# Dot and cross products of the gathered vectors on VectorE instead of GpSimd, in the last stage of a four-layer graph network

## The chip, the core and the metric

One Trainium2 chip, one of its cores. The metric is the device time of one execution of the whole program in microseconds. One core has a matrix engine (TensorE; PE, and PEld for its weight loads), a vector engine (VectorE; DVE), a scalar engine (ScalarE; ACT), GpSimd (POOL) and SyncE (SP), which only issues transfers here.

## The reference

12,500 nodes with 32 features, and 412,500 directed edges that are sorted by their destination. Four graph layers follow one another, each with a residual sum and a layer norm. The change touches the fourth layer alone:

```python
src, dst = (edge_index[0], edge_index[1])
R = jax.nn.relu(abs_distances[:, None] @ w1 + b1) @ w2 + b2      # 384 radial weights an edge
Y = spherical_harmonics(rel_vec)
Fj = features[src]                                               # gathered rows: 8 scalars, 8 vectors
...
acc = acc + _NORM[i] * jnp.einsum('euv,ef,evi,ofi->euo', Rb[..., k], Yf, Fb, C)
...
out = out.at[dst].add(msg)
```

`features` is x after three layers, `abs_distances` the edge weight, `rel_vec` a direction with three components. Of each gathered node the 32 features are 8 scalars and 8 vectors of three. With the real coupling tensors the sum falls into a few kinds of terms: scalars, vectors, the dot product of each vector with the unit direction, the cross product of each vector with it, and the direction times a weighted sum.

## The kernel before

The program runs in this order: preparation, a stage over all edges for layer 1 that also builds an adjacency image (`edges_and_adjacency`), ten propagation steps on that image and layer 3 (`propagate`), and the last stage, `tensor_messages`. That one takes the edges in NG = 324 groups of 10 tiles of 128 edges. Groups alternate between two sets of buffers (`m` = 0 or 1). The programs of the engines are written out by hand and meet at semaphores; a loop turn (`Fori`) is one pair of groups. For group n:

- SP loads edge weights, destinations and unit directions (`load`, L1551 to L1553). For group n this waits until the rows of group n-2 are ready (`rows_ready`), so a load starts when VectorE finishes a group. The indices are loaded separately (L1543).
- GpSimd gathers the source nodes by ten indirect transfers of one tile each (`gather`, L1500), and after the gather of group n+1 it makes the products of group n (`features`, L1503 to L1522): three multiplications of 128x240 elements (`pool_t`), one addition, one subtraction and one more addition, which write dot products and cross products into `m_features`. It waits for `loaded` and for ScalarE's `copied`, and signals `features_ready`.
- ScalarE makes the hidden radial layer (L1586), copies the gathered features into `m_features` and into `f1_cyclic`, the vectors with two components repeated (L1592 to L1595, signals `copied`), and builds the one-hot matrix of destinations (L1603, L1607).
- TensorE makes the radial weights, 384 an edge, in five batches of two tiles (`radial`, L1631), and sums the messages into the 128 nodes of a block with the one-hot matrix (`product`, L1636). The product of group n-1 is done within group n: tile 0 after batch 1, the nine others after batch 4. A group whose edges reach into a second block of nodes needs one more pass of ten tiles for it (`further_visits`).
- VectorE (`group`, L1756 to L1789) waits for `features_ready`, multiplies the radial weights of each batch by the features (L1766 once, L1770 three times a batch), drains its pipeline (L1774), sums (L1775), adds a finished block (`add`, L1730 and L1733), makes the one-hot matrix of a second block where there is one (L1737), sums again (L1778), keeps the destinations (L1783), and completes the rows (L1785, L1789), which signals `rows_ready`.

A batch buffer of the radial weights is one of two halves: TensorE may write batch b once VectorE has used batch b-2 (`r_used`).

Of the kernel before, what the change touches and what calls it, by code (L numbers as in the profile page):

```python
# [21 lines left out]
F32 = mybir.dt.float32  # L22
# [4 lines left out]
ALU = mybir.AluOpType  # L27
ACT = mybir.ActivationFunctionType
AX = mybir.AxisListType
# [6 lines left out]
EP = P  # L36
G = 10
# [3 lines left out]
NG = E // GE  # L41
PAIRS = NG // 2
# [39 lines left out]
def view(ap, offset, dims):  # L82

    return bass.AP(ap.tensor, ap.offset + offset, [list(ap.ap[0])] + [list(d) for d in dims])
# [13 lines left out]
def await_alone(eng, passed, sem, value):  # L98


    eng.wait_ge(sem, value)
    eng.sem_inc(passed, 1)
# [1317 lines left out]
def tensor_messages(nc, k, s):  # L1420
# [6 lines left out]
    sb, pb, sem, io = k.sb, k.pb, k.sem, k.io  # L1427
    U = 8
# [14 lines left out]
    unit = [sb(f"m_unit{m}", [EP, G, 5], F32, s) for m in range(2)]  # L1443

    FX = 8 * U
    feat = [sb(f"m_features{m}", [EP, G, FX], F32, s) for m in range(2)]
    cyclic = [sb(f"f1_cyclic{m}", [EP, G, U, 5], F32, s) for m in range(2)]
    pool_t = [sb(f"pool_t{n}", [EP, G, U, 3], F32, s) for n in range(3)]


    RW = 2 * U + 1
# [16 lines left out]
    loaded = [sem(f"m_loaded{m}") for m in range(2)]  # L1468
    idx_loaded = [sem(f"m_idx_loaded{m}") for m in range(2)]
    gathered = [sem(f"m_gathered{m}") for m in range(2)]  # L1470
    hid_ready, r_ready, r_used = sem("m_hid_ready"), sem("m_r_ready"), sem("m_r_used")
    copied, pool_step, features_ready = sem("m_copied"), sem("m_pool_step"), sem("m_features_ready")
    rows_ready, features_used = sem("m_rows_ready"), sem("m_features_used")
    extra_ready, rows_free = sem("m_extra_ready"), sem("m_rows_free")
    product_done, added = sem("m_product_done"), sem("m_added")
# [12 lines left out]
    with ExitStack() as q:  # L1488
        r_ps = pb("radial_ps", [EP, 2, RB, 512], F32, q)
        v_ps = pb("m_visit_ps", [P, 3, 512], F32, q)  # L1490
        with nc.Block() as block:

            @block.gpsimd
            def _(pool):
                def gather(i, m, first):
                    await_alone(pool, k.passed_pool, idx_loaded[m], (i + 1) * 16)
                    if not first:
                        await_alone(pool, k.passed_pool, copied, i * 2 + (m - 1))
                    for j in range(G):
                        pool.indirect_dma_start(src[m][:, j, :], None, k.x3_d,  # L1500
                                                bass.IndirectOffsetOnAxis(idx[m][:, j:j + 1], 0)).then_inc(gathered[m], 16)

                def features(n, turn, m, first):  # L1503

                    mul = lambda to, a, b: nc.gpsimd.tensor_tensor(to, a, b, ALU.mult).then_inc(pool_step, 1)
                    shifted = lambda at: view(cyclic[m][:], at, [[5 * U, G], [5, U], [1, 3]])
                    r_o = lambda at: view(unit[m][:], at, [[5, G], [0, U], [1, 3]])
                    await_alone(pool, k.passed_pool, loaded[m], turn * 48)
                    if not first:
                        await_alone(pool, k.passed_pool, features_ready, n)  # L1510
                    await_alone(pool, k.passed_pool, copied, n + 1)
                    mul(pool_t[0][:], shifted(0), r_o(0))
                    mul(pool_t[1][:], shifted(2), r_o(1))
                    mul(pool_t[2][:], shifted(1), r_o(2))
                    part = lambda i: view(pool_t[0][:], i, [[3 * U, G], [3, U]])
                    s_out = view(feat[m][:], U, [[FX, G], [1, U]])
                    await_alone(pool, k.passed_pool, pool_step, n * 5 + 3)
                    nc.gpsimd.tensor_tensor(s_out, part(0), part(1), ALU.add).then_inc(pool_step, 1)
                    nc.gpsimd.tensor_tensor(view(feat[m][:], 3 * U, [[FX, G], [1, U], [2 * U, 3]]), pool_t[1][:], pool_t[2][:],
                                            ALU.subtract).then_inc(pool_step, 1)  # L1520
                    await_alone(pool, k.passed_pool, pool_step, n * 5 + 5)
                    nc.gpsimd.tensor_tensor(s_out, s_out, part(2), ALU.add).then_inc(features_ready, 1)  # L1522
                gather(0, 0, True)
                gather(0, 1, True)
                features(0, 1, 0, True)
                with pool.Fori(1, PAIRS) as i:
                    gather(i, 0, False)
                    features(i * 2 - 1, i, 1, False)
                    gather(i, 1, False)
                    features(i * 2, i + 1, 0, False)  # L1530
                features(NG - 1, PAIRS, 1, False)

            @block.sync
            def _(sp):
# [155 lines left out]
            def _(dve):  # L1690
                tt, ts, red = nc.vector.tensor_tensor, nc.vector.tensor_scalar, nc.vector.tensor_reduce
# [47 lines left out]
                def visits(m, drained=False):  # L1739
# [5 lines left out]
                    with dve.If(end - block > 1):  # L1745
                        with dve.Fori(block + 1, end) as b:
# [6 lines left out]
                            dve.reg_add(extra_used, extra_used, 3)  # L1753
                            dve.reg_add(count, count, 1)

                def group(i, m, first):  # L1756
                    n = i * 2 + m
                    fe = feat[m][:]
                    dve.wait_ge(features_ready, n + 1)
                    if not first:  # L1760
                        dve.wait_ge(rows_free, n - 1)
                    for b in range(NBAT):
# [16 lines left out]
                    table_first, table_end = blocks(dve, n)  # L1779
                    dve.reg_mov(first_r, table_first)  # L1780
                    dve.reg_mov(end_r, table_end)
                    dve.wait_ge(loaded[m], (i + 1) * 48)
                    nc.vector.tensor_copy(kept[m][:], dst[m][:])  # L1783
                    dve.drain()  # L1784
                    tt(view(turned_along[:], 0, [[3 * U, G], [U, 3], [1, U]]), view(along[:], 0, [[U, G], [0, 3], [1, U]]),  # L1785
# [52 lines left out]
```

## Time and profile before

| | |
|---|---|
| median of 3 runs | 15099.62 us |
| lowest and highest | 15078.14 and 15099.76 us |
| span of the profiled execution | 18914.5 us |
| busy in it: PE, DVE, ACT, POOL | 14494.5, 10873.1, 5258.0, 7506.3 us |
| last stage in it, from 12619 to 18871 us | 6252 us for 324 groups |

The profiled execution is 3815 us longer than the median of the undisturbed runs. Its durations and orders are what can be read; how the difference is spread over the stages the profile does not say. In the rows below, times are microseconds from the start of the span, a row of a timeline merges equal instructions that follow each other ("x3"), and what stands in brackets is the time for which the engine stood idle before, with what ended it. "issue" means that nothing in the profile explains the idle time, "remote" that a semaphore moved and no recorded instruction moved it. PE work is listed by its matmul instructions, two for one tile in this type.

### The profile page before, as it was taken

To read this page: it belongs to the slowest core of one execution; us is meant where nothing else is said; L and a number is where in the kernel's file an instruction comes from. 1 tells how busy PE (TensorE), PEld (TensorE's weight loads), DVE (VectorE), ACT (ScalarE), POOL (GpSimd) and SP (SyncE) were. 2 spreads that over 40 slices of the span, in tenths; PEclk is the share of its full clock that TensorE was granted. 3 is DMA by queue.
4 is the path that set the end of the run, shared out by engine and by line. 5 is a ranking of instruction groups with operands and counts; after the bars stand their busy time and mean duration, and the time that the engine had idled before them with its cause. 6 is when DMAs were issued, how large, how long until landed. Compare 5 with 4: busy or idle time off the path is not lost. (4 is left out here: it accounts for less than half of the span.)

```text
span 18914.5 us, 402579 instructions
## 1 busy us (share of the span) xinstructions
PE 14494.5 (77%) x139778; PEld 9671.3 (51%) x139779; DVE 10873.1 (57%) x15415; ACT 5258.0 (28%) x10677; POOL 7506.3 (40%) x8530
## 2 busy tenths in 40 slices
PE   2666666666666666799999999977787778777877
PEld 2555555555555555655555555544444444444444
DVE  6444444444444444455555555557787777777777
ACT  2333333333333333100000000014444444444443
POOL 4444444444444444000000000026676666666765
PEclk8666666666666666699999999989999999999999
DMA  2100010101010010165666566541111111111111
GB/s 72 23 21 22 21 22 20 23 20 23 21 23 21 21 23 21 60 190 187 190 188 190 188 191 190 171 122 27 27 28 28 28 27 28 28 27 27 28 27 27
DMA packets 1143323, 1240.77 MB, mean 66 GB/s; under 512 B 399134, under 2 KB 1111834, under 8 KB 1142394
## 3 DMA queue, kind: packets, MB, share of 16 engines
q1 hardware_dynamic: 932485, 1124.29, 19.8%
q0 software_dynamic: 210496, 113.01, 4.2%
q14 instruction: 259, 2.11, 0.0%
q8 instruction: 83, 1.36, 0.0%
HBM read 1143.04 MB, written 93.60 MB: 65 GB/s over the span
## 5 line engine op out<-in xcount | busy, mean ns | idle before, releaser
L1500 POOL DMA_INDIRECT m_src<-x_after_layer,m_idx x3240 | 3130.8, 966 | 6032.8 <-DMA m_idx<-in_src 4921.4
L180 POOL DMA_INDIRECT l_xin<-in_x,l_idx x3240 | 3095.0, 955 | 4382.1 <-DMA l_idx<-in_src 3211.4
L1232 PE MATMUL p_prod<-a_slot,f_parts 128*32 128x448 fp8e4 x90552 | 4318.4, 353 | 105.4 <-DVEq L1397 50.6
L1232 PEld LDWEIGHTS p_prod<-a_slot,f_parts 128*32 128x32 bf16 x90552 | 2428.9, 97 | 1932.8 <-issue 115.6
L1631 PE MATMUL radial_ps<-radial_w,radial_hidden 128*128 128x384 f32 x6480 | 2598.2, 538 | 719.1 <-DVE m_products L1770 420.0
L581 PE MATMUL a_ps<-hot_hi,hot_lo 128*128 128x196 bf16 x6272 | 1640.4, 303 | 1902.7 <-ACT a_image L680 958.9
L749 DVE TENSOR_TENSOR hot_hi<-window_hi,number_ps 128x1568 bf16<-128x1568 f32 x784 | 1401.2, 1787 | 2895.4 <-PE degree_ps L582 1502.9
L1636 PE MATMUL m_visit_ps<-m_products,m_onehot 128*128 128x288 f32 x8420 | 2445.4, 440 | 561.8 <-DVE m_onehot L1737 261.8
L1636 PEld LDWEIGHTS m_visit_ps<-m_products,m_onehot 128*128 128x128 f32 x8420 | 1669.8, 201 | 1370.3 <-issue 767.9
L1631 PEld LDWEIGHTS radial_ps<-radial_w,radial_hidden 128*128 128x128 f32 x6480 | 1212.8, 202 | 1992.9 <-issue 793.3
L680 ACT ACTIVATE a_image<-a_ps 128x392 fp8e4<-128x392 f32 x3136 | 1478.5, 496 | 2644.6 <-PE a_ps L581 1672.3
L1314 DVE TENSOR_SCALAR a_slot<-a_nibbles 128x1568 int32<-128x1568 int32 x1085 | 1059.3, 976 | 1953.6 <-PE p_prod L1232 992.0
L581 PEld LDWEIGHTS a_ps<-hot_hi,hot_lo 128*128 128x128 bf16 x6272 | 720.3, 115 | 2339.5 <-issue 1133.7
L1770 DVE TENSOR_TENSOR m_products<-radial_ps,m_features 128x256 f32<-128x256 f32 x4860 | 1745.6, 415 | 0.0
L1766 DVE TENSOR_TENSOR m_products<-radial_ps,m_features 128x512 f32<-128x512 f32 x1620 | 1113.6, 687 | 1078.0 <-PE radial_ps L1631 453.5
L582 PE MATMUL degree_ps<-hot_hi,hot_lo 128*128 128x196 bf16 x6272 | 1659.5, 306 | 9.1 <-issue 9.0
L1603 ACT ACTIVATE m_difference<-m_nodes,m_dst 128x128 f32 x3240 | 982.9, 389 | 2459.3 <-PEq L1656 1590.6
L622 PE MATMUL e_visit_ps<-e_onehot,e_hidden 128*97 x8420 | 1369.8, 335 | 352.5 <-ACT e_hidden L693 169.9
L622 PEld LDWEIGHTS e_visit_ps<-e_onehot,e_hidden 128*97 128x97 f32 x8420 | 1313.7, 216 | 426.7 <-issue 420.0
L611 PE MATMUL h_ps<-w1a,xt 49*128 49x96 f32 x6480 | 1271.1, 357 | 262.6 <-issue 132.8
L611 PEld LDWEIGHTS h_ps<-w1a,xt 49*128 49x128 f32 x6480 | 1127.5, 260 | 451.0 <-issue 450.8
L1270 ACT ACTIVATE turned<-p_prod,digit_weight 128x448 f32<-128x448 f32 x154 | 97.7, 635 | 4254.0 <-PE p_prod L1232 4254.0
(203 smaller groups left out, 12640.4 us busy)
## 6 DMA issues: line engine op xcount, KB each, us to landing
a_nibbles<-multiplicity_digit SPq DMA_DIRECT2D x1085, 784.0 KB, 4.4
edge_w<-in_edge_weight SPq DMA_DIRECT2D x324, 320.0 KB
multiplicity_digit<-a_packed SPq DMA_DIRECT2D x392, 196.0 KB
l_xin<-in_x,l_idx POOLq DMA_INDIRECT x3240
m_src<-x_after_layer,m_idx POOLq DMA_INDIRECT x3240
xt<-in_edge_attr SPq DMA_DIRECT2D x324, 80.0 KB, 2.2
edge_directions<-rel_unit SPq DMA_DIRECT2D x12, 675.0 KB
m_unit<-edge_directions SPq DMA_DIRECT2D x324, 25.0 KB
```

Of the source, the lines that this page charges most:

```text
L180: pool.indirect_dma_start(k.xin[m][:, j, :], None, k.io["x"], bass.IndirectOffsetOnAxis(k.idx[m][:, j:j + 1], 0)).then_inc(k.gathered[m], 16)
L581: counts = nc.tensor.matmul(a_ps[:, bank, v * WC:(v + 1) * WC], lo, hot_hi[batch % 2][:, w, :], start=True, stop=True)
L582: mm = nc.tensor.matmul(degree_ps[:, 0:WC], lo, hot_hi[batch % 2][:, w, :], start=False, stop=False, skip_group_check=True)
L611: mm = nc.tensor.matmul(h_ps[:, t * DH:(t + 1) * DH], xt[:, m % 2, (b * HT + t) * EP:(b * HT + t + 1) * EP], w1a[:], start=True, stop=True)
L622: mm = nc.tensor.matmul(visit_ps[:, 0:P], hid[m % 2][:, j, :], view(onehot[:], (v % 2) * (G * P) + j * P, [[1, P]]), start=(j == 0), stop= ...
L680: nc.scalar.activation(view(image[:], h * (NB * QW) + 4 * l, [[QW, NB], [1, 4]]).bitcast(FP8), view(a_ps[:], l % 2 * 512, [[1, NB], [NB, 4 ...
L749: tt(hot_hi[b % 2][:], view(k.window_hi[:, bass.ds(at, WB)], 0, [[1, WB], [0, WC]]), view(numbers, 0, [[0, WB], [1, WC]]), ALU.is_equal)
L1232: mm = nc.tensor.matmul(view(prod[rows, w, :], 0, [[QW, 2], [1, QW]]), source[:, h * HH + j, r * D:(r + 1) * D], slots[h][:, 2 * w:2 * w + ...
L1500: pool.indirect_dma_start(src[m][:, j, :], None, k.x3_d, bass.IndirectOffsetOnAxis(idx[m][:, j:j + 1], 0)).then_inc(gathered[m], 16)
L1631: mm = nc.tensor.matmul(r_ps[:, half, t, 0:RD], hid[m][:, b * RB + t, :], w2[:], start=True, stop=True)
L1636: mm = nc.tensor.matmul(view(v_ps[:], (v % 3) * 512, [[U + 1, D], [1, U + 1]]), onehot[one][:, j, :], view(prod[m][:], j * PW + FIRST, [[R ...
L1770: mul = tt(view(prod[m][:], t0 * PW + LONG + o * U * RW + 1, [[PW, RB], [RW, U], [1, 2 * U]]), view(r_ps[:], at + 4 * U * U, [[512, RB], [ ...
```

## The change

GpSimd's `features` and its semaphores (`pool_step`, `features_ready`) are gone; GpSimd only gathers. VectorE has a function `features` of five instructions and two drains, called at the head of each group after waits for `loaded` and `copied`. The sum of three products is one reduction instead of two additions. The wait for `loaded` further down in the group is gone, since it now stands at the head.

```diff
@@ GpSimd
-                def features(n, turn, m, first):
-                    mul = lambda to, a, b: nc.gpsimd.tensor_tensor(to, a, b, ALU.mult).then_inc(pool_step, 1)
-                    ...
-                features(0, 1, 0, True)
                 with pool.Fori(1, PAIRS) as i:
                     gather(i, 0, False)
-                    features(i * 2 - 1, i, 1, False)
                     gather(i, 1, False)
-                    features(i * 2, i + 1, 0, False)
-                features(NG - 1, PAIRS, 1, False)
@@ VectorE
+                def features(m):
+
+                    shifted = lambda at: view(cyclic[m][:], at, [[5 * U, G], [5, U], [1, 3]])
+                    r_o = lambda at: view(unit[m][:], at, [[5, G], [0, U], [1, 3]])
+                    tt(turned_f[0][:], shifted(0), r_o(0), ALU.mult)
+                    tt(turned_f[1][:], shifted(2), r_o(1), ALU.mult)
+                    tt(turned_f[2][:], shifted(1), r_o(2), ALU.mult)
+                    dve.drain()
+                    red(view(feat[m][:], U, [[FX, G], [1, U]]), turned_f[0][:], AX.X, ALU.add)
+                    tt(view(feat[m][:], 3 * U, [[FX, G], [1, U], [2 * U, 3]]), turned_f[1][:], turned_f[2][:], ALU.subtract)
+                    dve.drain()
+
                 def group(i, m, first):
                     n = i * 2 + m
                     fe = feat[m][:]
-                    dve.wait_ge(features_ready, n + 1)
+                    dve.wait_ge(loaded[m], (i + 1) * 48)
+                    dve.wait_ge(copied, n + 1)
+                    features(m)
                     if not first:
                         dve.wait_ge(rows_free, n - 1)
...
                     dve.reg_mov(end_r, table_end)
-                    dve.wait_ge(loaded[m], (i + 1) * 48)
                     nc.vector.tensor_copy(kept[m][:], dst[m][:])
```

## Rows read from the trace of the kernel before

**Rows 1.** The stage's stretch: length, each engine's busy time (instructions), clock, DMA share, GB/s

```profile
12619.00:18871.00 6252.00, 4958.87 (x14884) 2878.36 (x14884) 4874.98 (x9049) 2654.98 (x5184) 4310.97 (x5184) 0.93 0.14 27
```

**Rows 2.** Waits in the stage's stretch: who for whom, us in total, times, longest

```profile
POOL pool_t L1505 <- ACT f_cyclic L1595: 626.2, 159, 13.7
DVE m_products L1766 <- PE radial_ps L1631: 453.5, 277, 7.0
DVE m_products L1766 <- issue: 294.8, 126, 5.4
DVE m_products L1766 <- remote: 273.8, 103, 7.7
PE m_visit_ps L1636 <- DVE m_onehot L1737: 261.8, 97, 6.6
```

**Rows 3.** Timeline of VectorE, second half of a group with one block, and next head

```profile
15040.03 0.69 DVE L1766 TENSOR_TENSOR m_products<-radial_ps,m_features 128x512 f32<-128x512 f32 x1
15040.64 1.08 DVE L1770 TENSOR_TENSOR m_products<-radial_ps,m_features 128x256 f32<-128x256 f32 x3
15041.84 1.49 DVE L1775 TENSOR_REDUCE m_along<-m_products 128x80 f32<-128x1280 f32 x1
15043.25 0.45 DVE L1730 TENSOR_REDUCE m_visit<-m_visit_ps 128x32 f32 x1
15043.86 0.19 DVE L1733 TENSOR_TENSOR m_sums<-m_sums,m_visit 128x32 f32 x1 [0.17 <-issue]
15044.35 2.82 DVE L1778 TENSOR_REDUCE m_products<-m_products 128x320 f32<-128x2560 f32 x1 [0.30 <-issue]
...
15047.33 0.41 DVE L1785 TENSOR_TENSOR m_turned_along<-m_along,m_unit 128x240 f32<-128x240 f32 x1
15047.81 0.58 DVE L1789 TENSOR_TENSOR m_products<-m_products,m_turned_along 128x240 f32<-128x240 f32 x1
15048.31 0.68 DVE L1766 TENSOR_TENSOR m_products<-radial_ps,m_features 128x512 f32<-128x512 f32 x1
...
15049.90 0.68 DVE L1766 TENSOR_TENSOR m_products<-radial_ps,m_features 128x512 f32<-128x512 f32 x1
```

**Rows 4.** Timeline of VectorE after groups with a second block: one-hot, next heads

```profile
15021.97 1.49 DVE L1737 TENSOR_TENSOR m_onehot<-m_dst_kept,m_nodes 128x1280 f32<-128x1280 f32 x1 [0.55 <-issue]
...
12747.60 0.69 DVE L1766 TENSOR_TENSOR m_products<-radial_ps,m_features 128x512 f32<-128x512 f32 x1 [3.67 <-issue]
...
18840.80 0.69 DVE L1766 TENSOR_TENSOR m_products<-radial_ps,m_features 128x512 f32<-128x512 f32 x1 [4.05 <-PE radial_ps L1631]
```

**Rows 5.** Timeline of TensorE: the extra pass of that group and what follows

```profile
15023.96 5.33 PE L1636 MATMUL m_visit_ps<-m_products,m_onehot 128*128 128x288 f32 x20 [2.65 <-DVE m_onehot L1737]
15030.03 2.84 PE L1631 MATMUL radial_ps<-radial_w,radial_hidden 128*128 128x384 f32 x8 [0.74 <-issue]
```

**Rows 6.** Groups by line and shape, 13400 to 18800 us: busy, mean ns, idle before

```profile
L1733 DVE TENSOR_TENSOR m_sums<-m_sums,m_visit 128x32 f32 x367 | 121.9, 332 | 61.0 <-issue 61.0
L1737 DVE TENSOR_TENSOR m_onehot<-m_dst_kept,m_nodes 128x1280 f32<-128x1280 f32 x85 | 134.6, 1584 | 26.4 <-issue 15.4 <-PE m_visit_ps L1636 10.5
```

**Rows 7.** Durations by line, ns: least, median, most; L1785 and L1505 from 13400 to 18800 us

```profile
L1785 DVE TENSOR_TENSOR m_turned_along<-m_along,m_unit x281: 407/409/475, 13407.9 to 18784.4; 128x240 f32<-128x240 f32 x141
L1505 POOL TENSOR_TENSOR pool_t<-f_cyclic,m_unit x843: 681/707/2024, 13418.4 to 18796.1; 128x240 f32<-128x240 f32 x169
L1733 DVE TENSOR_TENSOR m_sums<-m_sums,m_visit x420: 191/193/1301, 12684.1 to 18866.2; 128x32 f32 x140
```

**Rows 8.** Timeline of GpSimd: a whole turn, first and last of ten gathers

```profile
15042.37 0.98 POOL L1500 DMA_INDIRECT m_src<-x_after_layer,m_idx  x1 [0.46 <-issue]
...
15053.86 0.95 POOL L1500 DMA_INDIRECT m_src<-x_after_layer,m_idx  x1 [0.30 <-DMA m_unit<-edge_directions]
15057.76 2.04 POOL L1505 TENSOR_TENSOR pool_t<-f_cyclic,m_unit 128x240 f32<-128x240 f32 x3 [2.95 <-ACT f_cyclic L1595]
...
15061.14 0.38 POOL L1522 TENSOR_TENSOR m_features<-m_features,pool_t 128x80 f32<-128x80 f32 x1 [0.18 <-POOL m_features L1519]
15062.47 0.99 POOL L1500 DMA_INDIRECT m_src<-x_after_layer,m_idx  x1 [0.94 <-issue]
```

**Rows 9.** Timeline of ScalarE: last copy for the group that starts at 15048.31

```profile
15037.61 0.36 ACT L1595 COPY f_cyclic<-m_src 128x160 f32<-128x160 f32 x1
```

More of the change, by code:

```diff
@@ L1447, in tensor_messages @@
     cyclic = [sb(f"f1_cyclic{m}", [EP, G, U, 5], F32, s) for m in range(2)]
-    pool_t = [sb(f"pool_t{n}", [EP, G, U, 3], F32, s) for n in range(3)]
+    turned_f = [sb(f"turned_f{n}", [EP, G, U, 3], F32, s) for n in range(3)]
     RW = 2 * U + 1
@@ L1471, in tensor_messages @@
     hid_ready, r_ready, r_used = sem("m_hid_ready"), sem("m_r_ready"), sem("m_r_used")
-    copied, pool_step, features_ready = sem("m_copied"), sem("m_pool_step"), sem("m_features_ready")
+    copied = sem("m_copied")
     rows_ready, features_used = sem("m_rows_ready"), sem("m_features_used")
@@ L1501, in gather @@
                                                 bass.IndirectOffsetOnAxis(idx[m][:, j:j + 1], 0)).then_inc(gathered[m], 16)
-                def features(n, turn, m, first):
-                    mul = lambda to, a, b: nc.gpsimd.tensor_tensor(to, a, b, ALU.mult).then_inc(pool_step, 1)
[L1506 to L1522, printed above, removed]
                 gather(0, 0, True)
                 gather(0, 1, True)
-                features(0, 1, 0, True)
                 with pool.Fori(1, PAIRS) as i:
                     gather(i, 0, False)
-                    features(i * 2 - 1, i, 1, False)
                     gather(i, 1, False)
-                    features(i * 2, i + 1, 0, False)
-                features(NG - 1, PAIRS, 1, False)
             @block.sync
```

## The prediction

> **What bounds the kernel now.** I read the windows first, then the waits, then the timelines. The change touches only the last stage, 6252 us of the profiled span for 324 groups, 19.3 us a group. In it PE is busy 79%, DVE 78%, POOL 69% [rows 1]: three engines are nearly full, and the shares don't say which one sets the pace.
>
> The cycle of each, without waits, does. VectorE: a batch takes 1.59 us (15049.90 - 15048.31), and there are four; the last batch with its drain takes 1.81 (15041.84 - 15040.03); L1775 1.41; the adding of a block 1.10 (15044.35 - 15043.25); L1778 to the next head 3.96 (15048.31 - 15044.35). Together 14.6 us [rows 3]. A second block costs it about 3.2 more (a one-hot of 1.49 us with its gaps, and a second adding of about 1.1), and 97 of the 324 groups have one [rows 2, 4], so 15.6 us on average. GpSimd: the ten gathers take 12.44 us (15053.86 + 0.95 - 15042.37), the products 3.76 (15061.14 + 0.38 - 15057.76), the step to the next gather 0.94: 17.1 us [rows 8]. That is more than VectorE's, but its products wait another 626 us, 1.9 us a group, for ScalarE's copies [rows 2], so in this execution GpSimd isn't the bound.
>
> What VectorE waits for at the heads of groups decides the matter. I measured from the end of each L1789 to the start of the next L1766. In the 226 intervals after a group without a second block the mean is 0.1 us, 24 us in all; [rows 3] show one, where the head follows at once. In the 97 after a group with one the mean is 3.66 us, none is under 1.0 and 90 are over 2.3; first 3.67, last 4.05 [rows 4]. Their cause is TensorE: the extra one-hot is made late on VectorE, TensorE waits for it, runs 5.33 us, and only then makes the first radial weights of the next group [rows 5]. So in seven heads of ten VectorE sets the pace, and in three TensorE.
>
> **The change part by part.** *Added on VectorE.* Three multiplications of 128x240. L1770 x3 shows what such a series costs: 1.08 us for three of 256 elements, of which the first two steps take (1.08 - 0.41)/2 = 0.33 each; a step that ends in a drain takes 0.48, as L1785 (15047.81 - 15047.33) [rows 3]. That gives 0.33 + 0.33 + 0.48 = 1.14 us. The reduction of 240 elements to 80: no row shows it; I take the step of 0.33, bounded above by 0.45, the reduction L1730. The subtraction writes with a stride as L1789 does, 0.58, or takes 0.41 as L1785. Behind it comes a drain, and the sequencer must then take up the waits for `rows_free` and `r_ready`: after L1733 such a passage cost 0.30 [rows 3]. I take 0.83 for the two. Sum 1.14 + 0.33 + 0.83 = 2.3 us a group. Bounds: five steps of 0.33 without a cost of the drains, 1.65; five of 0.58, 2.9. The chosen value is nearest to rows with the same shape and the same drain.
>
> *Where it counts.* In 226 groups nothing covers it: 226 x 2.3 = 520 us. In 97 it lies in the wait for TensorE and costs about 5 us in all (seven heads under 2.3). That cover holds because the whole of group n, its one-hot of the second block too, moves with VectorE, and TensorE's lag behind it stays as it is. If the cover were gone, 97 x 2.3 = 223 us more. Within the group nothing absorbs the delay: batches 0 and 1 wait ready in both halves, and later batches wait for `r_used`, which moves too.
>
> *Removed from GpSimd.* 3.76 us a group of 17.1, and the chain from copies over products to the head. On VectorE this gives back the wait for `features_ready`: in heads with no second block before them at most the 24 us above. In the others it hid in TensorE's time.
>
> *Less collision.* L1733 takes 193 ns in the median and up to 1301 [rows 7], 332 in the mean [rows 6]; L1737 1.49 alone [rows 4] and 1.584 in the mean [rows 6]. Both read two inputs from SBUF, and by their start times 156 of the 158 L1733 over 250 ns overlap a product of GpSimd. Gone: 423 x 0.139 + 97 x 0.09 = 68 us.
>
> *Moved waits.* `loaded` and `copied` at the head: the last copy for the group that starts at 15048.31 is over at 15037.97 [rows 9], 10 us before. While such a wait lasted, all of VectorE's group, `r_used` and `rows_ready` would be queued behind it, and TensorE and SP's loads would wait for those; with 10 us of slack I cost it at nothing. The gather of group n+2 still starts at `copied` of group n, and earlier than now, since no products stand before it. The removed wait at L1783 had long been met: nothing.
>
> *GpSimd undisturbed.* The undisturbed runs are 3815 us shorter than this execution. If VectorE and TensorE run more freely there, GpSimd's 17.1 us come closer to being the bound, and removing 3.76 of them gives something back. The rows show only that it is near. Bounds: 0, and 1.5 us (17.1 - 15.6) in 226 groups, 340 us. I take 45, near zero, since the heads without a second block show almost no wait.
>
> Sum: 520 + 5 - 24 - 68 - 45 = +388 us, which is 19,300 on the profiled span of 18,914.5. On the undisturbed median: 15,099.6 + 388, rounded 15,490. I add the same microseconds there, since all added work is VectorE's own. A difference of 0.2%, 30 us, is about what a measurement of this kernel can tell from no change.
>
> **A rule against the change.** L1785, the nearest instruction to the new ones (two inputs in SBUF, 240 elements), ran beside GpSimd's gathers at 407 to 475 ns in all 281 records [rows 7, 8]: no gather delays it. The Trainium skill, SBUF — State Buffer, section "SBUF: two separate sides", says that GpSimd and a VectorE instruction with two SBUF inputs exclude each other on shared ports when the GpSimd operation reads SBUF, whichever starts first holding them for its whole length. If a gather counted as such an operation, the four new two-input instructions would each be held up; the trace does not show it.
>
> **The rivals.** (A) Faster: undisturbed, GpSimd is the bound. Its cycle then is 17.1 plus the wait for copies, up to 19.0; after the change VectorE sets 15.6 + 2.3 = 17.9, less 0.2 for collisions. From a present undisturbed cycle of 17.7 on, the change gains; at 18.4, in the middle, it gives 0.7 x 324 = 230, so 14,870. For it: 17.1 is above 15.6, and TensorE's waits may be shorter undisturbed. Against: heads without a second block show 0.1 us of wait. (B) TensorE sets the pace in far more groups than the heads show, since VectorE waits 1022 us in all at L1766 [rows 2], 355 + 24 of them at the heads counted above; the 643 us within groups, 2.0 us a group, might take up much of the delay. That gives 0 to half of the sum, 15,100 to 15,290. Against: a wait within the group comes from a batch that itself waits for `r_used`. (C) No cover: the extra one-hot comes later and TensorE's wait, 262 us in 97 groups now, grows with it; all 324 groups pay, 745 - 137 = +608, so 15,710. (D) Locking: each of four new instructions is held for half a gather of 0.95 us, in 226 groups 4 x 0.48 x 226 = 434 more, 15,920. It is the outcome of the rule above. (E) The change moves work, but VectorE's new work is hidden everywhere: this is (B) at its lower end.
>
> **How the numbers follow.** Forecast 0.64, between 15,300 and 15,650 by the bounds of 1.65 and 2.9 us. (A) 0.12, (B) 0.14, half of it within 30 us, (C) 0.07, (D) 0.03. The range of 15,180 to 15,710 leaves out A, D and the lower end of B, under 2 in 10. Faster 0.12, same 0.07, slower 0.81.
>
> **What the profile after would show.** Five new lines on VectorE at each head, 2.3 us from first start to L1766 in groups after a one-block group; head waits for TensorE shorter by that much after the others, about 1.3 us left; L1733 near 193 ns in the mean; POOL's share down by some 1250 us; the stage near 6640 us of the span. If the new instructions take over 0.5 us each, (D) holds; if the waits for TensorE at L1766 stay as long after groups with a second block, (C); if the stage grows by less than 150 us and waits within groups shrink, (B). I am wrong in sign if the stage is shorter.

## The result, and the profile after

| | median, us | lowest to highest | last stage, us | granted clock in it |
|---|---|---|---|---|
| before | 15097.29 | 15078.14 to 15099.76 | 5574 (run e0_before) | 0.98 |
| after | 15829.74 | 15825.21 to 15834.63 | 6346 | 0.90 |

The change makes the kernel slower, ratio 1.049 (95% interval 1.0475 to 1.0505), by 732 us. I had forecast 388 us. The sign was right; the size was half of what it came to, and the time lies outside my range of 15,180 to 15,710.

The profile shown ahead of the prediction was of a disturbed execution, 18,914 us long (one of the ten runs of e0_before, at 24,264 us, was disturbed too); a profile of the same kernel on an undisturbed one (e0_before, span 15,086.8 us) takes its place in every comparison below.

The last stage from its first to its last message instruction, first after, then e0_before. The columns are those of [rows 1]:

```profile
9441.00:15787.00 6346.00, 5080.71 (x14872) 2966.11 (x14872) 5412.22 (x10652) 2644.85 (x5172) 3155.76 (x3227) 0.90 0.15 27
```

```profile
9469.00:15043.00 5574.00, 4728.33 (x14872) 2733.69 (x14872) 4884.71 (x9037) 2647.72 (x5160) 4285.66 (x5158) 0.98 0.16 31
```

The stage grew by 772 us; everything ahead of it and behind it together took 28 us less. VectorE has 528 us more to do and GpSimd 1130 less. TensorE has the same 14,872 instructions and is busy for 352 us more. Its clock has two levels, 1.2 and 2.4 GHz; a mean grant of 0.98 means that 4% of the stage passed at the lower one, 0.90 that 19% did. By the clock intervals in the two traces that is 201 us before and 1212 after.

After: VectorE from the end of one group to its third batch, at a head with no second block before it. Answers to [rows 3]:

```profile
12016.89 0.58 DVE L1778 TENSOR_TENSOR m_products<-m_products,m_turned_along 128x240 f32<-128x240 f32 x1
12017.50 0.41 DVE L1736 TENSOR_TENSOR turned_f<-f_cyclic,m_unit 128x240 f32<-128x240 f32 x1
12017.82 0.40 DVE L1737 TENSOR_TENSOR turned_f<-f_cyclic,m_unit 128x240 f32<-128x240 f32 x1
12018.14 0.40 DVE L1738 TENSOR_TENSOR turned_f<-f_cyclic,m_unit 128x240 f32<-128x240 f32 x1
12018.62 0.40 DVE L1740 TENSOR_REDUCE m_features<-turned_f 128x80 f32<-128x240 f32 x1
12018.94 0.55 DVE L1741 TENSOR_TENSOR m_features<-turned_f 128x240 f32<-128x240 f32 x1
12019.74 0.69 DVE L1756 TENSOR_TENSOR m_products<-radial_ps,m_features 128x512 f32<-128x512 f32 x1 [0.25 <-issue]
...
12021.34 0.68 DVE L1756 TENSOR_TENSOR m_products<-radial_ps,m_features 128x512 f32<-128x512 f32 x1
...
12024.38 0.69 DVE L1756 TENSOR_TENSOR m_products<-radial_ps,m_features 128x512 f32<-128x512 f32 x1 [1.37 <-PE radial_ps L1607]
```

The new work takes 2.24 us from first start to the first batch (12017.50 to 12019.74). Then, at batch 2, VectorE waits 1.37 us for TensorE: that is new. TensorE in the same group, after:

```profile
12014.32 2.84 PE L1607 MATMUL radial_ps<-radial_w,radial_hidden 128*128 128x384 f32 x8 [0.73 <-issue]
12017.92 0.77 PE L1612 MATMUL m_visit_ps<-m_products,m_onehot 128*128 128x288 f32 x2 [0.75 <-DVE m_products L1778]
12021.48 6.20 PE L1607 MATMUL radial_ps<-radial_w,radial_hidden 128*128 128x384 f32 x12 [2.79 <-DVE m_products L1760]
```

and in e0_before:

```profile
12014.43 0.77 PE L1636 MATMUL m_visit_ps<-m_products,m_onehot 128*128 128x288 f32 x2 [0.75 <-DVE m_products L1789]
12015.86 3.15 PE L1631 MATMUL radial_ps<-radial_w,radial_hidden 128*128 128x384 f32 x8 [0.67 <-DVE m_products L1770]
12019.20 1.56 PE L1631 MATMUL radial_ps<-radial_w,radial_hidden 128*128 128x384 f32 x4 [0.19 <-DVE m_products L1770]
```

Before, TensorE stood idle for 0.67 us ahead of batch 2, did batches 2 and 3 in 3.15 us and batch 4 in 1.56. After, it stood idle for 2.79 us, since both halves were full and VectorE was making features, and then the same twelve instructions took 6.20 us. Over the groups after a one-block group, 224 of 226 with complete records, the wait ahead of batch 2 went from 0.60 to 2.64 us in the median, and that ahead of tile 0 stayed at 1.07 and 1.06. The granted clock of that stretch, and of a neighbouring one (columns: length, PE busy and instructions, granted clock, DMA share, GB/s):

```profile
12018.00:12025.00 7.00, 4.21 (x8) 0.76 0.32 59
12001.90:12008.00 6.10, 6.06 (x10) 0.51 0.03 3
```

In the second one the clock is at its lower level all through: start to start, matmul instructions of 384 columns lie 0.64 us apart there and 0.32 elsewhere. The Trainium skill, TensorE: Matmul & The Clock Gate, section "HAM oscillation — how this bites in real kernels", describes this pattern, an engine that goes idle between bursts and begins each burst cold. This trace agrees in the pattern: 2.8 us of waiting, then 0.64 us a matmul instruction. It does not agree in the size: the idle stretches that the section blames are longer than these.

The little that the kernel before loses to the lower clock lies mostly elsewhere, in the extra pass for a second block, which follows a wait for the one-hot. At full clock that pass takes 5.33 us [rows 5]; in e0_before 40 of the 97 take over 5.6, like this one:

```profile
9654.45 6.94 PE L1636 MATMUL m_visit_ps<-m_products,m_onehot 128*128 128x288 f32 x20 [2.18 <-DVE m_onehot L1737]
```

Sorted by whether VectorE made the one-hot of a second block in the group before ("after two") or not, mean us of VectorE. The head runs from the end of the last instruction of a group to its first batch, the new work included; the waits are those ahead of batches 2 and 3 (a negative one is an overlap); the rest of the group is not shown:

| | groups | head | batch 2 | batch 3 | whole group |
|---|---|---|---|---|---|
| e0_before, after one block | 226 | 0.09 | 0.13 | -0.05 | 16.78 |
| after, after one block | 226 | 2.17 | 1.28 | 0.46 | 20.24 |
| e0_before, after two | 97 | 3.16 | 0.06 | -0.08 | 18.22 |
| after, after two | 97 | 3.04 | 0.06 | -0.08 | 18.11 |

226 x 3.46 - 97 x 0.11 = 771 us, the whole growth of the stage. Of the 3.46, 2.08 are work at the head and 1.66 are waits for a slow TensorE; the rest of a group gives 0.28 back. The 0.11 come from the extra pass, 5.98 us in the mean before and 5.84 after.

### The profile page after: what moved, and what is told of

The parts are those of the page before. It is cut to its first block and busy times, and to the rows that moved or that the text cites. A ratio compares the mean times of both kernels' runs of the same rounds, so it can differ in the third digit from the quotient of the medians.

```text
span 15830.9 us, 400157 instructions
## 1 busy us (share of the span) xinstructions
PE 13477.7 (85%) x139778; PEld 8853.0 (56%) x139779; DVE 11417.9 (72%) x17035; ACT 5159.2 (33%) x10677; POOL 6467.6 (41%) x6586
## 5 line engine op out<-in xcount | busy, mean ns | idle before, releaser
L1500 POOL DMA_INDIRECT m_src<-x_after_layer,m_idx x3240 | 3175.9, 980 | 8060.4 <-DMA m_idx<-in_src 4922.8
L1607 PE MATMUL radial_ps<-radial_w,radial_hidden 128*128 128x384 f32 x6480 | 2825.9, 585 | 832.3 <-DVE m_products L1760 648.4
L1612 PE MATMUL m_visit_ps<-m_products,m_onehot 128*128 128x288 f32 x8420 | 2339.1, 426 | 437.5 <-DVE m_products L1778 224.4
L1607 PEld LDWEIGHTS radial_ps<-radial_w,radial_hidden 128*128 128x128 f32 x6480 | 1381.8, 226 | 2185.4 <-DVE m_products L1760 1050.5
L1314 DVE TENSOR_SCALAR a_slot<-a_nibbles 128x1568 int32<-128x1568 int32 x1085 | 1058.9, 976 | 1957.4 <-PE p_prod L1232 984.8
L581 PE MATMUL a_ps<-hot_hi,hot_lo 128*128 128x196 bf16 x6272 | 1348.2, 267 | 225.8 <-ACT a_image L680 117.6
L582 PE MATMUL degree_ps<-hot_hi,hot_lo 128*128 128x196 bf16 x6272 | 1342.3, 264 | 0.0
L1562 ACT ACTIVATE radial_hidden<-edge_w,radial_w 64x1280 f32<-64x1280 f32 x324 | 868.3, 2680 | 1014.7 <-DMA m_unit<-edge_directions 981.9
L622 PE MATMUL e_visit_ps<-e_onehot,e_hidden 128*97 x8420 | 1028.6, 278 | 186.7 <-DVE e_total L760 138.9
L611 PE MATMUL h_ps<-w1a,xt 49*128 49x96 f32 x6480 | 963.0, 298 | 194.0 <-ACT xt L687 194.0
L622 PEld LDWEIGHTS e_visit_ps<-e_onehot,e_hidden 128*97 128x97 f32 x8420 | 948.0, 166 | 278.6 <-issue 277.4
L1315 DVE TENSOR_SCALAR a_slot<-a_nibbles 128x1568 int32<-128x1568 int32 x1085 | 1051.9, 969 | 0.0
```

The source lines that it names most:

```text
L581: counts = nc.tensor.matmul(a_ps[:, bank, v * WC:(v + 1) * WC], lo, hot_hi[batch % 2][:, w, :], start=True, stop=True)
L582: mm = nc.tensor.matmul(degree_ps[:, 0:WC], lo, hot_hi[batch % 2][:, w, :], start=False, stop=False, skip_group_check=True)
L622: mm = nc.tensor.matmul(visit_ps[:, 0:P], hid[m % 2][:, j, :], view(onehot[:], (v % 2) * (G * P) + j * P, [[1, P]]), start=(j == 0), stop= ...
L1500: pool.indirect_dma_start(src[m][:, j, :], None, k.x3_d, bass.IndirectOffsetOnAxis(idx[m][:, j:j + 1], 0)).then_inc(gathered[m], 16)
L1607: mm = nc.tensor.matmul(r_ps[:, half, t, 0:RD], hid[m][:, b * RB + t, :], w2[:], start=True, stop=True)
L1612: mm = nc.tensor.matmul(view(v_ps[:], (v % 3) * 512, [[U + 1, D], [1, U + 1]]), onehot[one][:, j, :], view(prod[m][:], j * PW + FIRST, [[R ...
```

## The experiments

Medians of 4 to 10 runs. "One" and "two" are the mean lengths of the groups after one block and after two. "Slow groups" are the groups after one block in which TensorE spent more than 1 us of batches 2 to 4 at the lower clock, out of 224 or 225 with complete records.

| run | time, us | ratio to before (95%) | stage | clock | one | two | slow groups |
|---|---|---|---|---|---|---|---|
| after, for comparison | 15,829.74 | 1.0490 (1.0475 to 1.0505) | 6346 | 0.90 | 20.24 | 18.11 | 222 |
| e0_before | 15,085.90 | 1.0002 (0.9992 to 1.0012) | 5574 | 0.98 | 16.78 | 18.22 | 15 |
| e1_no_products | 15,005.87 | 0.9948 (0.9931 to 0.9964) | 5524 | 0.98 | 16.53 | 18.27 | 8 |
| e2_pe_filler | 15,686.22 | 1.0399 (1.0382 to 1.0416) | 6191 | 0.98 | 18.59 | 20.35 | 0 |
| e3_between5 | 15,854.06 | 1.0512 (1.0494 to 1.0529) | 6367 | 0.93 | 18.95 | 21.33 | 22 |
| e4_split | 15,907.57 | 1.0542 (1.0525 to 1.0560) | 6410 | 0.90 | 20.46 | 18.23 | 224 |
| e5_dot_only | 15,448.97 | 1.0242 (1.0225 to 1.0259) | 5954 | 0.94 | 18.13 | 18.98 | 101 |
| e6_tail | 15,841.61 | 1.0499 (1.0482 to 1.0517) | 6345 | 0.91 | 20.02 | 18.58 | 218 |
| e7_between3 | 15,611.67 | 1.0347 (1.0329 to 1.0364) | 6125 | 0.97 | 18.70 | 19.40 | 14 |
| e8_before_early | 15,031.33 | 0.9963 (0.9950 to 0.9977) | 5512 | 0.98 | 16.91 | 17.26 | 54 |
| e9_after_early | 15,747.90 | 1.0438 (1.0424 to 1.0452) | 6246 | 0.91 | 20.15 | 17.29 | 215 |
| e10_after_early_between3 | 15,485.63 | 1.0263 (1.0247 to 1.0279) | 5986 | 0.99 | 18.54 | 18.36 | 5 |
| e11_before_add_first | 15,199.66 | 1.0072 (1.0058 to 1.0085) | 5662 | 0.96 | 17.83 | 16.67 | 109 |

**e0_before.** No edit.

> The kernel before, unchanged, for a profile of an execution as long as the undisturbed ones: the recorded one is 3815 us longer, that of the changed kernel (15,831 us) is not. Theory 1 (clock): the 732 us are about 520 us of new work on VectorE in groups with nothing to cover it, and the rest comes from TensorE, which now idles 2.6 us while VectorE makes the features, and then runs matmuls at half clock (0.64 us instead of 0.32). It expects in the undisturbed kernel before far less time at half clock in the last stage than the 1251 us after the change, under 900. Theory 2 (work alone): 324 x 2.26 us = 732 us, since no head has a cover when undisturbed; it expects head waits near zero after groups with a second block too, and time at half clock like that after the change. Time about 15,097.

The clock speaks for theory 1: 201 us of the stage at the lower level, not 1212. So do the heads after a second block: 3.16 us of wait, with no products on VectorE, against theory 2's zero. What this profile also corrects is GpSimd. It waits for ScalarE's copies for 39 us in the whole stage, not 626 [rows 2]:

```profile
POOL pool_t L1505 <- ACT f_cyclic L1595: 38.8, 39, 13.0
```

It is full almost without a break, as my 17.1 us a turn suggested: 4286 us of instructions, 1086 of idle time that nothing explains and 116 between its own dependent steps fill 5488 of the 5574 us. The chain of work that ended last passes through it too (L1500 with 12.1% of the stage, L1505 with 4.2%). The profile alone can't say what that is worth; the next run, with its theory 3, measures it.

**e1_no_products.** The products are left out on every engine after the first two groups.

```diff
-                    features(m)
+                    if first:
+                        features(m)
```

> The changed kernel with the dot and cross products left out on every engine after the first two groups (stale values are used; all waits stay). VectorE is then as in the kernel before and GpSimd as after. Theories 1 and 2 both expect the 732 us back: 15,100. If GpSimd's products cost time in the kernel before, this is faster than that kernel by what they cost: theory 3 (GpSimd was near its bound) expects 14,700 to 15,000, from VectorE's cycle of 15.6 us with 1 us of waits against the 17.4 us a group that the kernel before takes undisturbed.

15,006 us, 0.5% under the kernel before. That is all that GpSimd's products cost there, about 75 us, its share of the bound and its collisions with VectorE together. Theory 3 had 14,700 to 15,000 and is missed by 6 us at its small end: the effect is there, and it is small. It lies in the groups after one block (16.53 against 16.78 us); those after two gain nothing (18.27 against 18.22). And VectorE's own products cost 824 us in the changed kernel, more than their length: 323 heads of 2.24 us would be 724, even with no cover at all, which is the most that theory 2 can give.

**e2_pe_filler.** Three matmuls whose result isn't used.

```diff
+                        if b == 1:
+                            for _ in range(3):
+                                nc.tensor.matmul(spare_ps[:, 0:RD], hid[m][:, 0, :], w2[:], start=True, stop=True)
```

> The changed kernel with three more matmuls of 384 columns (1.9 us) on TensorE in each group, into a spare bank, after product tile 0, where it now waits for VectorE. They compute nothing that is used. Theory 1: the clock stays up, the waits at batches 2 and 3 after heads (1.3 + 0.46 us in 226 groups, 393 us) vanish; in the 97 groups after a second block, where TensorE is behind, the filler costs up to 2 us each, 190 us: about 15,630, faster than the changed kernel by 200. Theory 2: work for TensorE can't help: the same time at best, up to 200 us longer: 15,830 to 16,030.

15,686 us: faster by 144 us with 323 x 1.9 us of useless work added to TensorE. The clock is back at 0.98. TensorE in a group after one block:

```profile
12035.11 0.77 PE L1613 MATMUL m_visit_ps<-m_products,m_onehot 128*128 128x288 f32 x2 [1.08 <-DVE m_products L1782]
12035.71 2.10 PE L1653 MATMUL spare_ps<-radial_w,radial_hidden 128*128 128x384 f32 x6
12038.49 1.56 PE L1608 MATMUL radial_ps<-radial_w,radial_hidden 128*128 128x384 f32 x4 [0.68 <-DVE m_products L1764]
```

Batch 2 comes in 1.56 us, at full clock, and VectorE's wait for it falls from 1.28 to 0.06 us. These groups go from 20.24 to 18.59 us (226 x 1.65 = 373 us back). The groups after two blocks, where TensorE is late anyway, pay for the filler: 18.11 to 20.35 (97 x 2.24 = 217 us), 1.7 us of it as a later batch 2 and 0.6 as a slower extra pass. The difference is 156 us, 144 measured. By order and dependence alone, more work on TensorE can't make VectorE wait less for it; the clock can. Theory 2 falls.

**e3_between5.**

```diff
-    BETWEEN = (1, 0, 0)
+    BETWEEN = (5, 0, 0)
```

> The changed kernel with five tiles of the product, not one, between radial batches 1 and 2: TensorE's own work fills the wait that the features made. Theory 1: time at half clock falls as with the filler, and the work is useful, so 15,830 - 393 + at most 97 x 2 = 15,550 to 15,650. Theory 2: order alone changes nothing, 15,830, or more where TensorE comes late with batch 2.

15,854 us: theory 1's number was missed by over 200. The profile shows why:

```profile
12013.29 2.84 PE L1607 MATMUL radial_ps<-radial_w,radial_hidden 128*128 128x384 f32 x8 [0.36 <-issue]
12019.27 3.97 PE L1612 MATMUL m_visit_ps<-m_products,m_onehot 128*128 128x288 f32 x10 [3.14 <-DVE m_products L1778]
12023.04 3.24 PE L1607 MATMUL radial_ps<-radial_w,radial_hidden 128*128 128x384 f32 x8
```

Useful work that is put into the idle time is missing from where it came from. TensorE ends the group four tiles earlier and now waits 3.14 us ahead of the product, and the product is what runs slow (ten instructions in 3.97 us; at full clock they take 2.70). The groups after one block still gain, 20.24 to 18.95, but those after two lose 3.2 us each: 1.8 because batch 2 comes after five tiles, and 1.5 because the extra pass, now behind a wait of 4.1 us for its one-hot, is slow in all 97 (7.30 us against 5.84). -292 + 312 = +20 us; measured +24.

**e4_split.** The three multiplications for the next group stand ahead of the long reduction, the rest stays at the head.

```diff
-                def group(i, m, first):
+                def group(i, m, first, ahead=True):
...
-                    dve.wait_ge(loaded[m], (i + 1) * 48)
-                    dve.wait_ge(copied, n + 1)
-                    features(m)
+                    features_end(m)
...
                         visits(1 - m, drained=True)
+                    if ahead:
+                        dve.wait_ge(loaded[1 - m], (i + 1 + m) * 48)
+                        dve.wait_ge(copied, n + 2)
+                        features(1 - m)
```

Here `features` holds the three multiplications and a drain, `features_end` the reduction, the subtraction and a drain.

> The changed kernel with its new work in two places: the three multiplications for the next group after the adding of a block, ahead of the long reduction, and the reduction to dot products and the subtraction at the head. The same instructions on the same engine, but TensorE's wait of 2.6 us becomes two of about half. Theory 1 (an idle stretch of 2.6 us on TensorE brings half clock behind it): the waits at batches 2 and 3 after heads, 1.28 + 0.46 us in 226 groups against about 0.05 before, go away, while both halves still lie behind the one-hot of a second block and stay covered there. 15,830 - 370 = 15,460 to 15,550. Theory 2 (work alone): 15,830, as the work is the same.

15,908 us, slower than the changed kernel, where I expected 300 less. The form of theory 1 in which one idle stretch of 2.6 us does the harm falls:

```profile
12005.61 0.77 PE L1612 MATMUL m_visit_ps<-m_products,m_onehot 128*128 128x288 f32 x2 [2.35 <-DVE m_products L1782]
12007.89 6.73 PE L1607 MATMUL radial_ps<-radial_w,radial_hidden 128*128 128x384 f32 x12 [1.51 <-DVE m_products L1760]
```

Two waits, 2.35 and 1.51 us, with 0.77 us of work between them, bring the lower clock just as well, in all 224 groups. What was right is the cover: in groups after two blocks both halves stay hidden (18.23 against 18.11).

**e5_dot_only.** The cross products are left out on every engine after the first two groups.

```diff
-                    tt(turned_f[1][:], shifted(2), r_o(1), ALU.mult)
-                    tt(turned_f[2][:], shifted(1), r_o(2), ALU.mult)
+                    if first:
+                        tt(turned_f[1][:], shifted(2), r_o(1), ALU.mult)
+                        tt(turned_f[2][:], shifted(1), r_o(2), ALU.mult)
...
-                    tt(view(feat[m][:], 3 * U, [[FX, G], [1, U], [2 * U, 3]]), turned_f[1][:], turned_f[2][:], ALU.subtract)
+                    if first:
+                        tt(view(feat[m][:], 3 * U, [[FX, G], [1, U], [2 * U, 3]]), turned_f[1][:], turned_f[2][:], ALU.subtract)
```

> The changed kernel with only the dot products made on VectorE (one multiplication, one reduction, two drains) and the cross products left out on every engine after the first two groups. About 1.2 us at the head instead of 2.1. Without any products the kernel took 15,006, with all of them 15,830: 824 us. If the cost were in proportion to the work, 1.2/2.1 of it, 470 us: 15,475. Theory 1: TensorE idles 1.6 us, too short for the clock to fall as often, so only 226 x 1.2 = 270 us: 15,280, and a time at half clock near 200 us, not 1219.

15,449 us, nearer to proportion than to 15,280. The head is 1.07 us in groups after one block; the clock is 0.94, half-way: a smaller fall, not none. Batches 2 to 4 are slow in 101 of 224 groups, such as this one:

```profile
12027.71 0.77 PE L1612 MATMUL m_visit_ps<-m_products,m_onehot 128*128 128x288 f32 x2 [1.11 <-DVE m_products L1780]
12029.94 5.83 PE L1607 MATMUL radial_ps<-radial_w,radial_hidden 128*128 128x384 f32 x12 [1.46 <-DVE m_products L1762]
```

Besides, the groups after two blocks are 0.7 us longer than without products, although their new work is hidden. That too is the clock: the extra pass is slow in 84 of 97 groups (6.72 us in the mean) and in 41 without products (6.01), and the head behind it is longer by just that, 3.93 us against 3.20. One such pass:

```profile
12077.46 6.94 PE L1612 MATMUL m_visit_ps<-m_products,m_onehot 128*128 128x288 f32 x20 [2.18 <-DVE m_onehot L1713]
```

**e6_tail.** All of the new work ahead of the long reduction; otherwise as e4_split, with nothing left at the head.

> The changed kernel with all of its new work, for the next group, after the adding of a block and ahead of the long reduction. TensorE's idle time moves as one piece from behind product tile 0 to ahead of it (0.6 + 2.1 us). Theory 1 in the form that the length of the idle stretch counts and not its place: again 15,750 to 15,850, with slow matmuls now in tile 0 and batch 2. If the place counts (batches 2 and 3 are what VectorE waits for, tile 0 isn't), 15,600 or less. Theory 2: 15,830.

15,842 us. The first form is right: place doesn't count much. TensorE idles 3.3 us (mean) ahead of tile 0 and 0.3 us behind it, and batch 2 is late again (1.17 us).

**e7_between3.** `BETWEEN = (3, 0, 0)`.

> The changed kernel with three product tiles between radial batches 1 and 2. Five tiles had moved the idle time from behind tile 0 (2.6 us) to ahead of it (2.7 us in the median) and it took 15,854 us. Three should split it in two stretches of 1.6 us. Theory 1: half clock goes, the 226 groups give back up to 1.7 us each, and batch 2 comes up to 1 us late in 97 groups: 15,830 - 380 + 97 = 15,550. Theory 2: 15,830 to 15,900.

15,612 us, 218 under the changed kernel and 62 over the forecast: groups after one block gain 1.54 us each, those after two lose 1.29. Two waits again, but with three tiles of work between them:

```profile
12020.87 1.78 PE L1612 MATMUL m_visit_ps<-m_products,m_onehot 128*128 128x288 f32 x6 [1.66 <-DVE m_products L1778]
12024.45 3.15 PE L1607 MATMUL radial_ps<-radial_w,radial_hidden 128*128 128x384 f32 x8 [1.81 <-DVE m_products L1760]
```

Batches 2 and 3 take 3.15 us, full clock. Against e4_split this proves little, since that run has the longer single wait (2.35 us). The run to set beside it is e5_dot_only. In the median TensorE waits there 1.0 us ahead of tile 0 and 1.5 ahead of batch 2, around 0.77 us of work, and 101 of 224 groups are slow; in e7 it waits 2.0 and 1.6 us, around 1.8 us of work, and 14 are. The waits of e7 are longer, and its clock stays up: the length of the waits alone doesn't decide. What differs besides is the work between them. No run here goes further into the rule.

**e8_before_early, e9_after_early and e10_after_early_between3.** The one-hot of a second block is made right behind the last batch. e8 is the kernel before with it, e9 the changed kernel, e10 the changed kernel with `BETWEEN = (3, 0, 0)` too.

```diff
+                def early(m):
+
+                    block, end = dve.snap(first_r, min_val=0, max_val=NB - 1), dve.snap(end_r, min_val=1, max_val=NB)
+                    with dve.If(end - block > 1):
+                        dve.wait_ge(product_done, dve.snap(extra_used, min_val=2, max_val=NG * NB))
+                        one_hot(onehot[2], m, dve.snap(first_r, min_val=0, max_val=NB - 2) + 1).then_inc(extra_ready, 1)
...
+                    if not (first and m == 0):
+                        early(1 - m)
                     dve.drain().then_inc(features_used, 1)
```

> The kernel before (products on GpSimd) with the one-hot matrix of a second block made right behind the last batch and not behind the adding of a block. It tests what the cover in the 97 groups is: TensorE waits 2.26 us for that one-hot, and VectorE waits 3.16 us at the next head for TensorE. If the late one-hot is the cause, the head wait falls to about 0.9 us, 97 x 2.2 = 210 us less: 14,870, faster than either kernel. If TensorE is the bound there by its own work, the time stays at 15,086.

> The same edit in the changed kernel. There the features already lie in that wait, of which only 0.8 us is left at the head (3.04 us less 2.2 of features). If the cover is what I take it for, only this rest can be gained: 97 x 0.8 = 78 us, less what the falling clock then costs in those groups as in the others (up to 1.6 us each, 155 us): 15,750 to 15,900, against 15,830. If cover and clock have nothing to do with it, 210 us as in the kernel before: 15,620.

> The changed kernel with the early one-hot and three product tiles between batches 1 and 2. With three tiles alone it took 15,612; the groups after a second block lasted 19.4 us, of which 3.61 us at the head. Early one-hot takes the wait for TensorE there, 1.4 us in 97 groups, 135 us: 15,480. It would show how near the change can come to the kernel before when TensorE is kept busy.

e8 takes 15,031 us, faster than both kernels, by 0.37% and not by 1.4%. TensorE's wait for the one-hot has given way to another:

```profile
PE m_visit_ps L1636 <- DVE m_sums L1733: 156.0, 97, 2.1
```

TensorE must not write a bank before VectorE has added its old content (`added`), and that comes behind the sum L1775. Heads after two blocks fall from 3.16 to 2.16 us, and the 97 groups give back 93 us. The groups after one block take about 30 of them again (16.78 to 16.91 us): the extra pass is hardly ever slow now, but batches 2 to 4 are in 54 groups and not in 15.

Nor did GpSimd leave much room: 4237 us of instructions, 1089 of unexplained idle time and 115 between its own steps fill 5441 of the 5512 us, and my 14,870 needed a stage of 5360. Whether it held this run back, no run here tells.

e9 gained 82 us: groups after two blocks go from 18.11 to 17.29, the 0.8 us that the features had left uncovered, as forecast, without a loss to the clock there; 17.29 is also what e8 has without the new work (17.26), so the addition is still covered in them.

e10 came at 15,486 (15,480 forecast) with the clock at 0.99. It is the changed kernel with both its troubles mended, and it is still 2.6% behind the kernel before: 400 us more than e0_before, 454 more than e8, which has the early one-hot too.

**e11_before_add_first.** The kernel before, with `visits` ahead of the sum L1775.

```diff
-                    red(along[:], view(prod[m][:], 1, [[PW, G], [RW, U], [1, 2 * U]]), AX.X, ALU.add)
                     if not (first and m == 0):
                         visits(1 - m, drained=True)
+                    red(along[:], view(prod[m][:], 1, [[PW, G], [RW, U], [1, 2 * U]]), AX.X, ALU.add)
```

> The kernel before (products on GpSimd) with the adding of a block, and with it the one-hot of a second block, ahead of the sum L1775 instead of behind it. The early one-hot alone gave 57 us, not 210, since TensorE then waited 1.6 us for the semaphore added, which L1733 moves behind the sum of 1.4 us. Here both come 1.4 us earlier. If those two are all that TensorE waits for in the 97 groups, its wait falls from 2.26 to about 0.9 us and the time by 97 x 1.4 = 136 us, to 14,950. If the wait only changes its cause again, 15,030 to 15,086.

15,200 us, slower, where I had 14,950. The groups after two blocks do what I expected, 18.22 to 16.67 (150 us). The 226 others pay 1.05 us each (237 us). The adding now stands right behind the drain, and VectorE is idle ahead of it 420 times with nothing in the profile to explain it, against 98 times and 43 us in e0_before:

```profile
DVE m_visit L1730 <- issue: 222.3, 420, 0.9
```

That is 0.5 us a group. The other half is the clock again, 0.96 instead of 0.98, 109 slow groups instead of 15, and a wait of 0.59 us at batch 2 that was 0.13. A delay of 0.5 us on VectorE cost twice its length here.

## Why the prediction was wrong in its size

*The new work, 2.3 us a head.* Right: 2.24 us from its first start to the first batch, 2.08 on the head. The pieces answer the rows they were taken from: multiplications 0.40 to 0.41 with steps of 0.32, the one with a drain 0.48, the reduction 0.40, the strided subtraction 0.556.

*226 heads pay, 97 don't.* Right, and the best part of it. The heads after two blocks are 3.04 us long with the new work inside, and were 3.16 without; rival C falls. The cover has two parts: making the one-hot earlier (e8) takes 1.0 us off it, adding the block earlier too (e11) brings it to 1.12, so about 2.0 of the 3.16 us come from VectorE's own order. In e9 the 2.16 that are left still hold the new work.

*Collisions.* Right as durations: L1733, 360 ns in the mean in e0_before, is 198 as L1709; L1737, 1654 ns, is 1494 as L1713. Together 423 x 0.16 + 97 x 0.16 = 83 us of VectorE's time, 68 forecast, though what falls in the groups after two blocks earns nothing, as e1 shows:

```profile
L1709 DVE TENSOR_TENSOR m_sums<-m_sums,m_visit 128x32 f32 x422 | 83.4, 198 | 71.2 <-issue 71.2
L1736 DVE TENSOR_TENSOR turned_f<-f_cyclic,m_unit 128x240 f32<-128x240 f32 x323 | 131.0, 405 | 3.7
```

All 186 of the L1733 in e0_before that take over 281 ns overlap a product of GpSimd, and those beside a gather alone take 193 ns. Rival D falls too: the multiplications take 402 to 405 ns in the mean, 873 of 969 of them beside a gather, and none over 468. So the exclusion that the Trainium skill, SBUF — State Buffer, section "SBUF: two separate sides", states is seen here between VectorE and GpSimd's arithmetic, and not between such a VectorE instruction and a gather.

*GpSimd near its bound.* 45 us for it, 24 for its semaphore and 68 for the collisions, 137 in all; e1_no_products gives 75. Rival A falls: in e0_before GpSimd's turn is as full as I feared, and yet it is worth under 1% of the time.

*"Within the group nothing absorbs the delay … later batches wait for `r_used`, which moves too."* This is the step that failed, and not in the direction that I weighed. I let TensorE shift by 2.3 us at no price. A shift means that it stands idle, for 2.8 us instead of 0.7, and an engine whose clock follows its activity then does the next batches at half speed. VectorE waits for those: 1.28 + 0.46 us instead of 0.13 - 0.05. Term missing from the sum: 226 x 1.66 = 375 us. With the other terms as measured (470 us at the heads, -11 after two blocks, -63 for the rest of a group) it makes the 771. Without it these terms are 396 us, next to my 388. That closeness is partly luck: at the heads I had 525 us where 459 were measured, and I let 137 be given back where it was 63.

There was a hint. [rows 1] give the stage a clock of 0.93, lower than the 0.98 of e0_before, and in the prediction the TensorE row is used for busy shares only. I also took the waits within groups, 2.0 us a group, for something that might *absorb* the delay (rival B). In e0_before they are about 0.1 us: there was nothing there to absorb it, and the question to ask was what TensorE does after it has waited.

The range of 15,180 to 15,710 took its upper end from rival C. Its bounds on VectorE's work were wide enough; a rival with another engine's reaction was missing.

## What to carry to other kernels

Where two engines hand work to each other batch by batch, work added to one can be idle time for the other, and in this kernel idle time on TensorE had a price of its own: count the added stall, look at the granted clock of the stretch behind it, and if it falls, add the slow matmuls that the first engine then waits for. Here 2.1 us at the head cost 3.5. To test for it, give the idle engine work that isn't needed; here the kernel got 144 us faster, which dependences alone can't bring about. And when a wait recurs only after certain groups, sort the heads by it before pricing: the 97 groups after a second block hid the whole addition, the 226 others hid nothing.

## What was not expected of the hardware

Waits of 2.6 us on TensorE ahead of batch 2, once a group of 20 us, with 1.1 us more ahead of tile 0, brought 19% of the stage to the lower clock; with 0.6 and 1.1 us it was 4%, most of that in the extra passes behind waits of 2.2 us. Cutting such a wait in two (2.35 and 1.51 us around 0.77 us of work) did not help; waits of 2.0 and 1.6 us around 1.8 us of work left the clock up in 210 of 224 groups. GpSimd could be busy without a break, 13.2 us of it recorded as instructions in groups of 17.2 us, and taking all its arithmetic away moved the time by 0.5% only.
